# Decoder layer on one core: the self-attention values first, the weight splits moved, one output tile joined in halves, and six transpositions of the identity at the start

## The chip, the core and the metric

The kernel runs on one core of one Trainium2 chip. The metric is the time of one execution on the device in microseconds (us). The engines are TensorE (PE in the profile, its weight loads PEld), VectorE (DVE), ScalarE (ACT), GpSimd (POOL) and SyncE (SP), which only issues DMAs. Each runs its own instructions in the order in which they are written and meets the others through semaphores.

## What is computed

A post-norm decoder layer for x of 2 x 256 rows of 512 and a context of 2 x 512 rows of 512, in float32. Cut to its core:

```python
# self-attention: 32 heads of 16, causal, with ALiBi
qkv = x @ w_attn + b_attn; q, k, v = split(qkv)
scores = q k^T / 16 + slope * (key - query), masked; attn = softmax(scores)
x = layernorm(x + (attn @ v) @ w_proj + b_proj)
# cross-attention: 32 query heads of 128, 8 key/value heads, keys from [context, x]
q = rms_norm(x @ Wq); k = rms_norm(kv @ Wk); v = kv @ Wv
x = layernorm(x + (softmax(q k^T / sqrt(128)) @ v) @ Wo)
# feed-forward per head of 32, on permuted columns
x = layernorm(x + unpermute(gelu(permute(x) @ up) @ down))
```

## The kernel before

Precision is kept by splitting a float32 matrix into a rounded high half and the rest as low half; one product is then three matmuls (`three_passes`, L46): high by high, high by low, low by high. Here a **triple** is such a set of three matmuls of 128x128 by 128x512. Four triples give a 128x512 result in one of the eight PSUM banks. ScalarE writes high halves (`weights_hi`), VectorE or GpSimd low halves (`early_lo`, `late_lo`).

**Start** (`self_attention_and_keys`, L213). SyncE loads the four row tiles of x (L351), then weights in groups of four 256 KB pieces numbered p: w_attn's queries (p = 0), keys (1), values (2), Wk in two halves (3, 4), Wv in two (5, 6), w_proj (7), Wq (8, 9). There is one raw buffer of four pieces, so a piece of group p is issued when the low half of the same piece of p - 1 is made (L339 to L343). TensorE transposes all of x (L802, 16 transpositions), waits for the last low half of x (L804), then does queries and keys (2 x 16 triples, the loop at L805), then walks a list.

**The list** is made by `order_of_work` (L82) and walked by all engines. Its entries: S c, the scores of a quad of four heads (16 quads, L833); E (c, i), the shift on VectorE (L628) and the exponential on ScalarE (L485) of head i; R, the reciprocals of sums (L637) after which GpSimd normalises two heads (L421, L423) and makes the ALiBi bias of two heads of the next quad (L416); T, transposition of a head's probabilities (L854) and its copy by VectorE (L643); PV, the product with the values (L866); V j, the values of row tile j (four triples); CT and CX, transposition and split of a tile of context (L876, L621); "part" (n, r), an eighth of the cross-attention keys and values of row n: two triples; KG and KT, copying and transposing those keys; W p, the split of weight group p. S c + 1 may not start before the shifts of all four heads of quad c are done (s_out, L835). T and the context transpositions share two banks in turn, bank 4 and bank 7: a use waits until the one two uses back is drained.

In the list the four V entries stand between the exponentials of quad 0; the parts begin after S 1, five to each quad.

**Cross-attention** (L1071 on) does eight key/value heads in turns of four units. In a unit TensorE transposes probabilities (T a, L1580), multiplies by values (O a) and, between them, does "fillers", among them the output product W tt of row tile tt with four triples. T, W and others share a ring of banks 4 to 6 (`Turn`, L1003). In the last turn (`LAST_FILLERS`) W 1 stands at the end of the last unit, after O 5; then come W 2, the transposition of row tile 0 (L1553), half of W 3, that of row tile 1, the other half. VectorE adds each to x (L1433) and makes the layer norm (L1436 to L1444).

**Feed-forward** (L1620 on) begins on TensorE at L1902: it waits for the permutation matrix, for the ring, and for `xt_lo` 2 (the low halves of row tiles 0 and 1, L1450), transposes row tile 2 (L1837) and permutes the columns by matmuls (L1849, L1850).

## Time and profile before

| | |
|---|---|
| runs of the kernel | 844.33, 845.17, 846.02 us; median 845.17 |
| the profiled execution | 845.65 us, its span 843.8 us |
| PE busy | 826.2 us (98%) |
| DVE, ACT, POOL busy | 547.2, 474.9, 521.9 us |
| DMA | 56.22 MB, mean 67 GB/s |

The span is what the profile covers; 1.85 us of the execution lie outside it. The trace's times count from the span's start. A matmul's duration is modelled and overlaps the next one's start, so the distance between the starts of two is what one costs the engine.

### The profile page before, as it was taken

What the parts mean: (1) busy time and instruction counts of PE and PEld (TensorE: products, weight loads), DVE (VectorE), ACT (ScalarE), POOL (GpSimd) and SP (SyncE); (2) the same over time, 40 slices, a digit from 0 to 9 for tenths busy, and PEclk for the clock granted to TensorE, in tenths of its full rate; (3) what the DMA queues carried; (4) which work ended last, traced back from release to release, by engine and by line L of the source; (5) the groups of instructions that cost most, each with busy time, mean ns of one, the idle gap of its engine ahead of it and who ended that gap; (6) DMA issues with size and microseconds to landing.
All of it is one profiled execution on the core that took longest, in us unless ns stands there. A gap on an engine that the chain in (4) does not pass through costs nothing.

```text
span 843.8 us, 15130 instructions
## 1 busy us (share of the span) xinstructions
PE 826.2 (98%) x4851; PEld 694.6 (82%) x4851; DVE 547.2 (65%) x1507; ACT 474.9 (56%) x1006; POOL 521.9 (62%) x676
## 2 busy tenths in 40 slices
PE   7999999999999999999999999999999999999997
PEld 5777777777788888888888888888888888888874
DVE  4456566766355677667767676667666766677664
ACT  4666665566246656455555555556555555556554
POOL 3477876757336576766666756775676576636931
PEclk9999999999999999999999999999999999999999
DMA  6613223221141721112102112122121101100101
GB/s 202 197 51 113 80 72 114 63 72 56 50 138 51 243 80 46 51 60 67 50 19 87 27 61 68 37 68 68 37 68 68 37 2 24 58 0 1 26 1 50
DMA packets 48511, 56.22 MB, mean 67 GB/s; under 512 B 4671, under 2 KB 29773, under 8 KB 48461
## 3 DMA queue, kind: packets, MB, share of 16 engines
q1 hardware_dynamic: 48460, 55.59, 21.6%
q8 instruction: 27, 0.44, 0.2%
q14 instruction: 24, 0.19, 0.1%
HBM read 41.95 MB, written 13.63 MB: 66 GB/s over the span
## 4 chain that ended last, share of the span: by engine, by line
PE 61%; DVE 3%; ACT 2%; POOL 0%; issue 0%; POOLq 0%
PE bank L1534 15%; PE bank L48 11%; PE bank L50 11%; PE bank L49 11%; PE bank L1580 9%; PE bank L1524 1%; ACT prob L1349 1%; DVE x_mx L1420 1%; ACT prob L1724 1%; DVE pT_lo L1469 0%; PE bank L1849 0%; PE bank L1850 0%; PE bank L1881 0%; PE bank L1891 0%; PE bank L1890 0%
## 5 line engine op out<-in xcount | busy, mean ns | idle before, releaser
L1251 POOL TENSOR_SCALAR prob<-prob,x_rinv 128x768 f32<-128x768 f32 x124 | 112.5, 908 | 167.4 <-DVE x_rinv L1429 167.4
L1366 ACT ACTIVATE pT_hi<-bank 128x512 fp32r<-128x512 f32 x192 | 114.2, 597 | 90.3 <-PE bank L1580 89.9
L1349 ACT ACTIVATE prob<-bank,x_nm,q_rms 128x768 f32<-128x768 f32 x124 | 123.2, 994 | 47.1 <-DVE x_nm L1423 46.7
L1469 DVE TENSOR_TENSOR pT_lo<-bank,pT_hi 128x512 fp32r<-128x512 f32 x192 | 130.3, 679 | 5.1 <-ACT pT_hi L1366 3.7
L1420 DVE TENSOR_REDUCE x_mx<-bank 128x1 f32<-128x768 f32 x124 | 118.3, 954 | 22.0 <-PE bank L1534 21.7
L1580 PE MATMUL bank<-ident,prob 128*128 128x128 f32 x768 | 114.8, 272 | 2.1 <-POOL prob L1251 1.3
L1580 PEld LDWEIGHTS bank<-ident,prob 128*128 128x128 f32 x768 | 95.0, 140 | 14.1 <-POOL prob L1251 2.0
L48 PE MATMUL bank<-pT_hi,xv_hi 128*128 128x512 f32 x192 | 86.5, 450 | 1.2 <-DVE pT_lo L1469 0.9
L485 ACT ACTIVATE s_self<-s_self,nm_self 128x128 f32<-128x128 f32 (+1 forms) x128 | 57.1, 447 | 43.0 <-DVE nm_self L628 42.5
L50 PE MATMUL bank<-pT_hi,xv_lo 128*128 128x512 f32 x192 | 75.7, 394 | 0.0
L49 PE MATMUL bank<-pT_lo,xv_hi 128*128 128x512 f32 x192 | 75.4, 393 | 0.0
L1534 PE MATMUL bank<-xk_hi,qT_hi 128*128 128x384 f32 x244 | 65.6, 350 | 0.3 <-ACT prob L1349 0.2
L1534 PE MATMUL bank<-xk_lo,qT_hi 128*128 128x384 f32 x244 | 63.4, 341 | 0.0
L1534 PE MATMUL bank<-xk_hi,qT_lo 128*128 128x384 f32 x244 | 62.7, 337 | 0.0
L48 PE MATMUL bank<-wq_hi,x_hi 128*128 128x512 f32 x144 | 58.8, 408 | 0.0
L1375 ACT ACTIVATE oT_hi<-bank 128x512 fp32r<-128x512 f32 x32 | 19.1, 598 | 69.5 <-PE bank L50 69.4
L50 PE MATMUL bank<-wq_hi,x_lo 128*128 128x512 f32 x144 | 56.5, 393 | 0.0
L49 PE MATMUL bank<-wq_lo,x_hi 128*128 128x512 f32 x144 | 56.4, 392 | 0.0
L48 PE MATMUL bank<-w_hi,cT_hi 128*128 128x512 f32 x128 | 56.0, 438 | 0.0
L643 DVE COPY pT_self<-bank 128x384 f32<-128x384 f32 x64 | 35.4, 554 | 29.3 <-PE bank L854 29.0
L48 PE MATMUL bank<-wo_hi,oT_hi 128*128 128x512 f32 x128 | 52.3, 409 | 0.0
L1534 PEld LDWEIGHTS bank<-xk_hi,qT_hi 128*128 128x128 f32 x244 | 43.5, 189 | 9.4 <-ACT prob L1349 1.5
(233 smaller groups left out, 2047.8 us busy)
## 6 DMA issues: line engine op xcount, KB each, us to landing
wo_raw<-in_Wo SPq DMA_DIRECT2D x8, 1024.0 KB, 5.4
v_by_head<-v_st SPq DMA_DIRECT2D x12, 512.0 KB, 3.5
kT_by_head<-kT_st SPq DMA_DIRECT2D x12, 512.0 KB, 3.2
xk_raw<-kT_by_head SPq DMA_DIRECT2D x16, 384.0 KB, 3.2
xv_raw<-v_by_head SPq DMA_DIRECT2D x16, 384.0 KB, 3.2
wq_raw<-in_Wq SPq DMA_DIRECT2D x6, 1024.0 KB, 5.5
wq_raw<-in_w_attn SPq DMA_DIRECT2D x12, 256.0 KB, 4.3
xk_raw<-in_ctx SPq DMA_DIRECT2D x8, 256.0 KB, 2.6
```

What stands on the lines that cost most here:

```text
L48: nc.tensor.matmul(out, a_hi, b_hi, start=first, stop=False)
L49: nc.tensor.matmul(out, a_hi, b_lo, start=False, stop=False)
L50: return nc.tensor.matmul(out, a_lo, b_hi, start=False, stop=last)
L485: nc.scalar.activation(s_sb[:, c % 2, i, a:e], s_sb[:, c % 2, i, a:e], ACT.Exp, bias=nm[:, c % 2, i, qt:qt + 1], scale=-1.0, accum_out=rsu ...
L643: nc.vector.tensor_copy(pT[:, c % 2, i, :], bank[:, bank_of("T", (c, i)), 0:3 * P]).then_inc(pt_out, 1)
L1251: nc.gpsimd.tensor_scalar(prob[:, s, :], prob[:, s, :], rinv[:, s:s + 1], 1.0, ALU.mult, ALU.mult)\
L1349: nc.scalar.activation(prob[:, s, :].rearrange("p (a e) -> p a e", a=2), bank[:, at:at + 2, 0:HALF], ACT.Exp, bias=nm[:, s:s + 1], scale=q ...
L1366: nc.scalar.activation(pT_hi[:, a, :], bank[:, turn.bank[s, what, a], :], ACT.Copy)\
L1420: nc.vector.reduce_max(mx[:, s:s + 1], bank[:, at:at + 2, 0:HALF], AX.XY)\
L1469: nc.vector.tensor_tensor(pT_lo[:, a, :], bank[:, turn.bank[s, what, a], :], f32(pT_hi[:, a, :]), ALU.subtract).then_inc(ring_out, 1)
L1534: last = nc.tensor.matmul(bank[:, at + c, 0:HALF], a_hi[:, g, w], k_part[:, b, c * HALF:(c + 1) * HALF], start=start, stop=stop)
L1580: last = nc.tensor.transpose(bank[:, at, j * P:(j + 1) * P], prob[:, UT * (s % 2) + j, a * P:(a + 1) * P], ident[:])
```

## The change

It makes these edits. (1) SyncE issues x and the weights of the values in turn (x 0, piece 0, x 1, ...), and the value weights come first; the context tile 0 is loaded before the key weights. (2) On TensorE the values are computed first, piece by piece between the row transpositions, with waits for one tile and one piece each instead of for all; six transpositions of the identity into bank 7, read by nobody, stand between those of row tiles 0 and 1. Queries and keys follow. (3) ScalarE and VectorE split x and the first weight group in turn. Groups 3 and 5 move from GpSimd to VectorE. (4) The values leave the list; the first four parts take their place between the exponentials of quad 0. In exchange the odd quads among the first eight lose one part each. From the group of S 9 on the list is as it was. (5) In the last turn W 1 becomes two halves in bank 3, outside the ring: WA (two triples) after T 1 of the last unit, WB after O 5. (6) In the feed-forward the wait for `xt_lo` 2 stands behind the transposition of row tile 2.

```diff
-    order = [("S", 0), ("W", 5), ("V", 0), ("E", (0, 0)), ("V", 1), ("E", (0, 1)), ("V", 2), ("E", (0, 2)), ("CT", 0), ("CX", 0), ("V", 3),
-             ("E", (0, 3)), ("R", (0, 0)), ("W", 6), ("R", (0, 1))]
+    order = [("S", 0)]
...
+    for i in range(QUAD):
+        parts(1)
+        order.append(("E", (0, i)))
+        if i % 2:
+            order.append(("R", (0, i // 2)))
+    order.append(("W", 6))
...
-        if c < NQ - 1:
+        if c not in (1, 3, 5, 7, NQ - 1):
             parts(1)
...
-        ON_VECTOR, ON_POOL = (0, 1, 2, 4, 6, 8), (3, 5, 7)
+        ON_VECTOR, ON_POOL = (0, 1, 2, 3, 4, 5, 6, 8), (7,)
...
-                name, g = (("w_attn", 0), ("w_attn", 1), ("w_attn", 2), ("Wk", 0), ("Wk", 1), ("Wv", 0), ("Wv", 1),
+                name, g = (("w_attn", 2), ("w_attn", 0), ("w_attn", 1), ("Wk", 0), ("Wk", 1), ("Wv", 0), ("Wv", 1),
                            ("w_proj", 0), ("Wq", 0), ("Wq", 1))[p]
                 for i in range(KT):
-                    if p > 0 and p - 1 in ON_VECTOR:
+                    if p == 0:
+                        sp.dma_start(x[:, i, :], d["x"].rearrange("b s d -> (b s) d")[tokens(i), :]).then_inc(x_in[i], 16)
+                    elif p - 1 in ON_VECTOR:
                         sp.wait_ge(w_los, KT * ON_VECTOR.index(p - 1) + i + 1)
...
             for j in range(TT):
                 act.wait_ge(xt_ps, j + 1)
                 nc.scalar.activation(xT_hi[:, :, tokens(j)], bank[:, j, :].rearrange("p (k t) -> p k t", k=KT), ACT.Copy)\
                     .then_inc(xt_hi, 1)
-            for i in range(KT):
-                weights_hi(0, i)
...
+                weights_hi(0, j)
             for i in range(KT):
                 weights_hi(1, i)
+            act.wait_ge(zeros, 2)
+            for j in range(TT):
+                take_values_of(j)
...
+            def values(i, j):
+
+                pe.wait_ge(xt_lo, j + 1)
+                pe.wait_ge(w_los, i + 1)
+                last = three_passes(nc, bank[:, 4 + j, :], xT_hi[:, i, tokens(j)], xT_lo[:, i, tokens(j)],
+                                    w_hi[:, 0, i, :], w_lo[:, 0, i, :], i == 0, i == KT - 1)
...
+            row_transposes(0)
+            for _ in range(6):
+                nc.tensor.transpose(bank[:, 7, 0:P], ident[:], ident[:])
+            row_transposes(1)
+            values(0, 0)
+            row_transposes(2)
+            for i, j in ((0, 1), (1, 0), (1, 1)):
+                values(i, j)
+            row_transposes(3)
+            for i, j in ((0, 2), (1, 2), (2, 0), (2, 1), (2, 2), (0, 3), (1, 3), (2, 3)):
+                values(i, j)
+            for j in range(TT):
+                values(KT - 1, j)
...
 LAST_FILLERS = ((("W", 2), ("QT", 2), ("QT", 3), None),
                 (("W", 3), None, None, None),
                 (None, None, None, ("W", 0)),
-                (None, None, None, ("W", 1)))
+                (("WA", 1), None, None, ("WB", 1)))
...
+            def second_output(heads):
+                pe.wait_ge(o_out, UNITS * (KVH - 1) + 2)
...
             pe.wait_ge(k.matrix_made, KT)
             pe.wait_ge(k.ring_out, k.ring_drained)
-            pe.wait_ge(xt_lo, 2)
...
             transposes(2)
+            pe.wait_ge(xt_lo, 2)
             permute(free[0], 0)
```

**Where instructions move.** TensorE at the very start; `x_rows` is x, `x_hi` and `w_hi` are halves of x and of a weight group. Before:

```order
L802 MATMUL bank<-ident,x_rows 128x128 x16
L48 MATMUL bank<-x_hi,w_hi 128x512
L49 MATMUL bank<-x_lo,w_hi 128x512
L50 MATMUL bank<-x_hi,w_lo 128x512
L48 MATMUL bank<-x_hi,w_hi 128x512
```

Now:

```order
L846 MATMUL bank<-ident,x_rows 128x128 x4
L861 MATMUL bank<-ident 128x128 x6
L846 MATMUL bank<-ident,x_rows 128x128 x4
L48 MATMUL bank<-w_hi,x_hi 128x512
L49 MATMUL bank<-w_lo,x_hi 128x512
L50 MATMUL bank<-w_hi,x_lo 128x512
L846 MATMUL bank<-ident,x_rows 128x128 x4
L48 MATMUL bank<-w_hi,x_hi 128x512
L49 MATMUL bank<-w_lo,x_hi 128x512
```

The first product now stands behind two row tiles' transpositions and the six of the identity.

TensorE in the last unit of the cross-attention, from its first transpositions (`prob`) on. Before:

```order
L1580 MATMUL bank<-ident,prob 128x128 x12
L48 MATMUL bank<-pT_hi,xv_hi 128x512
L49 MATMUL bank<-pT_lo,xv_hi 128x512
L50 MATMUL bank<-pT_hi,xv_lo 128x512
L1580 MATMUL bank<-ident,prob 128x128 x4
```

Now:

```order
L1647 MATMUL bank<-ident,prob 128x128 x8
L48 MATMUL bank<-wo_hi,oT_hi 128x512
L49 MATMUL bank<-wo_lo,oT_hi 128x512
L50 MATMUL bank<-wo_hi,oT_lo 128x512
L48 MATMUL bank<-wo_hi,oT_hi 128x512
L49 MATMUL bank<-wo_lo,oT_hi 128x512
L50 MATMUL bank<-wo_hi,oT_lo 128x512
L1647 MATMUL bank<-ident,prob 128x128 x4
L48 MATMUL bank<-pT_hi,xv_hi 128x512
L49 MATMUL bank<-pT_lo,xv_hi 128x512
```

Two triples of the output product of row tile 1 now stand before O 0 (the product of `pT_hi` and `xv_hi`); its other two stay behind O 5.

## Rows read from the trace of the kernel before

**Rows 1.** The page, busy time, share of the span, instructions of TensorE and its loads.

```profile
PE 826.2 (98%) x4851; PEld 694.6 (82%) x4851; DVE 547.2 (65%) x1507; ACT 474.9 (56%) x1006; POOL 521.9 (62%) x676
PEclk9999999999999999999999999999999999999999
```

**Rows 2.** Waits of TensorE: line, who it waited for, us in total, times, longest.

```profile
PE bank L802 <- DMA x_rows<-in_x: 3.4, 1, 3.4
PE bank L48 <- DVE w_lo L617: 2.1, 1, 2.1
...
PE bank L48 <- DVE pT_lo L1469: 0.9, 2, 0.8
```

**Rows 3.** Timeline, TensorE, first 20 us: start, us, engine, line, tiles.

```profile
3.45 3.73 PE L802 MATMUL bank<-ident,x_rows 128*128 128x128 f32 x16 [3.45 <-DMA x_rows<-in_x]
9.28 0.77 PE L48 MATMUL bank<-x_hi,w_hi 128*128 128x512 f32 x1 [2.10 <-DVE w_lo L617]
9.84 0.63 PE L49 MATMUL bank<-x_lo,w_hi 128*128 128x512 f32 x1
10.27 0.63 PE L50 MATMUL bank<-x_hi,w_lo 128*128 128x512 f32 x1
...
15.47 0.40 PE L49 MATMUL bank<-x_lo,w_hi 128*128 128x512 f32 x1
15.72 0.40 PE L50 MATMUL bank<-x_hi,w_lo 128*128 128x512 f32 x1
...
17.12 0.40 PE L50 MATMUL bank<-x_hi,w_lo 128*128 128x512 f32 x1
```

**Rows 4.** Timeline, ScalarE, the first high halves.

```profile
4.57 0.60 ACT L524 ACTIVATE x_hi<-bank 128x512 fp32r<-128x512 f32 x1 [2.54 <-PE bank L802]
...
7.70 2.18 ACT L474 ACTIVATE w_hi<-wq_raw 128x512 fp32r<-128x512 f32 x4
```

**Rows 5.** Timeline, VectorE, the first low halves.

```profile
5.20 0.69 DVE L675 TENSOR_TENSOR x_lo<-bank,x_hi 128x512 fp32r<-128x512 f32 x1 [3.63 <-ACT x_hi L524]
...
8.45 2.49 DVE L617 TENSOR_TENSOR w_lo<-wq_raw,w_hi 128x512 fp32r<-128x512 f32 x4
```

**Rows 6.** Busy time of each engine, clock, DMA share and GB/s, 2 to 8 us.

```profile
2.00:8.00 6.00, 3.73 (x16) 3.11 (x16) 2.23 (x4) 2.61 (x6) 5.26 (x7) 1.00 0.99 343
```

**Rows 7.** Timeline, VectorE, quads 0 to 2: group 6's and a context tile's low halves, a last shift.

```profile
49.90 2.83 DVE L617 TENSOR_TENSOR w_lo<-wq_raw,w_hi 128x512 fp32r<-128x512 f32 x4 [1.94 <-ACT w_hi L474]
...
61.30 0.68 DVE L621 TENSOR_TENSOR cT_lo<-bank,cT_hi 128x512 fp32r<-128x512 f32 x1
...
65.94 0.42 DVE L628 CUSTOM_DVE_ANT_0 s_self<-bank,alibi 128x256 f32<-128x256 f32 x1
```

**Rows 8.** Timeline, TensorE, scores of quads 2 and 3, a transposition of quad 4.

```profile
58.16 0.94 PE L844 MATMUL bank<-kT_even,qT 32*128 32x128 f32 x16 [0.52 <-DVE nm_self L628]
...
68.32 0.94 PE L844 MATMUL bank<-kT_odd,qT 32*128 32x128 f32 x16
...
98.68 0.55 PE L854 MATMUL bank<-ident,s_self 128*128 128x128 f32 x3 [0.25 <-POOL s_self L423]
```

**Rows 9.** Timeline, GpSimd, w_proj's low halves ahead of quad 4's second normalisation.

```profile
92.79 5.02 POOL L408 TENSOR_TENSOR wq_lo<-wq_raw,wq_hi 128x512 fp32r<-128x512 f32 x4
```

**Rows 10.** Timeline, TensorE, end of the cross-attention and the feed-forward's first rows.

```profile
793.09 1.47 PE L1580 MATMUL bank<-ident,prob 128*128 128x128 f32 x12
795.35 0.47 PE L48 MATMUL bank<-pT_hi,xv_hi 128*128 128x512 f32 x1 [0.79 <-DVE pT_lo L1469]
...
811.12 0.63 PE L1837 MATMUL bank<-ident,x_rows 128*128 128x128 f32 x4 [0.62 <-DVE x_lo L1450]
811.50 0.36 PE L1849 MATMUL bank<-x_hi,wq_hi 128*128 128x256 f32 x1
```

**Rows 11.** Timeline, VectorE, output of row tile 2 added, last low half.

```profile
806.90 0.69 DVE L1433 TENSOR_TENSOR x_rows<-bank,x_rows 128x512 f32<-128x512 f32 x1 [0.57 <-PE bank L50]
...
810.17 0.68 DVE L1450 TENSOR_TENSOR x_lo<-bank,x_hi 128x512 fp32r<-128x512 f32 x1
```

More of the change, by code:

```diff
@@ L283, in self_attention_and_keys @@
         RING, GROUPS = (4, 7), (5, 6)
-        before = {4: ("V", 0), 7: ("V", 3), 5: ("V", 1), 6: ("V", 2)}
-        place, quad, rows_over = {}, 0, {}
+        before = {4: ("K", 0), 7: ("K", 3), 5: ("K", 1), 6: ("K", 2)}
+        place, quad, rows_over = {("CT", 0): (1, None)}, 0, {}
         ring_uses = 0
@@ L520, in copy_keys, with take_values_of @@
                 nc.scalar.activation(k_sq[:], k_rows[:, w, :], ACT.Square).then_inc(ksq_made, 1)
+            def take_values_of(j):
+                act.wait_ge(v_ps, j + 1)
+                for odds in range(2):
+                    lanes = slice(odds * SA_DIM, (odds + 1) * SA_DIM)
+                    nc.scalar.activation(padded[odds][:, j, :, lanes],
+                                         bank[:, 4 + j, :].rearrange("p (g e) -> p g e", e=2 * SA_DIM)[:, :, lanes],
+                                         ACT.Copy).then_inc(v_out, 1)
             for j in range(TT):
@@ L676, in _, with odd_keys @@
                                         f32(xT_hi[:, :, tokens(j)]), ALU.subtract).then_inc(xt_lo, 1)
-            for p in range(2):
-                for i in range(KT):
-                    early_lo(p, i)
+                early_lo(0, j)
+            for i in range(KT):
+                early_lo(1, i)
+            def odd_keys(m):
+                dve.wait_ge(qk_ps, KT + m + 1)
+                dve.wait_ge(k_out, m + 1)
+                nc.vector.tensor_scalar(kT_odd[:, m, :], bank[:, 4 + m, :], cols[:, KT + m:KT + m + 1],
+                                        odd[:], ALU.add, ALU.mult).then_inc(k_odd_out, 1)
+            for i in range(KT):
+                early_lo(2, i)
             dve.wait_ge(col_out, 1)
@@ L685, in _ @@
             for i in range(KT):
-                early_lo(2, i)
-            for m in range(KT):
-                dve.wait_ge(qk_ps, KT + m + 1)
-                dve.wait_ge(k_out, m + 1)
-                nc.vector.tensor_scalar(kT_odd[:, m, :], bank[:, 4 + m, :], cols[:, KT + m:KT + m + 1],
-                                        odd[:], ALU.add, ALU.mult).then_inc(k_odd_out, 1)
-                early_lo(4, m)
+                early_lo(3, i)
+            early_lo(4, 0)
+            context_lo(0)
+            for i in range(1, KT):
+                early_lo(4, i)
+            odd_keys(0)
+            early_lo(5, 0)
+            early_lo(5, 1)
+            odd_keys(1)
+            early_lo(5, 2)
+            early_lo(5, 3)
+            odd_keys(2)
+            odd_keys(3)
             for what, a in ORDER:
@@ L796, in drained, with context_transposes, row_transposes @@
                     pe.wait_ge(vg_late, i[0] + 1)
-            pe.wait_ge(const, 4)
-            for j in range(TT):
+            def context_transposes(n):
+                pe.wait_ge(c_in, 16 * (n + 1))
+                if n > 0:
+                    drained("CT", n)
+                for i in range(KT):
+                    last = nc.tensor.transpose(bank[:, bank_of("CT", n), tokens(i)], c_raw[:, tokens(i)], ident[:])
+                last.then_inc(ct_ps, 1)
+            def row_transposes(j):
                 pe.wait_ge(x_in[j], 16)
@@ L870, in weigh_values @@
                 last.then_inc(o_ps, 1)
-            def context_transposes(n):
-                pe.wait_ge(c_in, 16 * (n + 1))
-                drained("CT", n)
-                for i in range(KT):
-                    last = nc.tensor.transpose(bank[:, bank_of("CT", n), tokens(i)], c_raw[:, tokens(i)], ident[:])
-                last.then_inc(ct_ps, 1)
             def key_transposes(n, g):
@@ L912, in _ @@
             for what, a in ORDER:
-                if what == "V":
-                    values(a)
-                elif what == "S":
+                if what == "S":
                     scores(a)
```

123 lines of the change are left out of this document (70 added, 53 removed).

## The prediction

> **What bounds the kernel now.** The page comes first: TensorE is busy 826.2 of 843.8 us, no other engine over 65% [rows 1]. So time can only come from three places: TensorE's waits, matmuls run slower than they could be, and work removed. The change removes no work (and adds six transpositions), so I look for the other two. The list of TensorE's waits says where it stands still: 3.4 us for the first tile of x, 2.1 us for the first low half of a weight, 0.9 us in two waits for a low half of the probabilities [rows 2], and 0.6 us ahead of the feed-forward [rows 10].
>
> The timeline of the start shows the other loss. From 9.84 to 10.27 one matmul of 512 columns costs 0.43 us; from 15.72 to 17.12 six cost 1.40 us, 0.235 us each [rows 3]. These are the two levels of the clock: 512 columns take 0.427 us at 1.2 GHz and 0.213 us at 2.4 GHz. The granted clock of the stretch reads full [rows 1, 6], so it is the spacing that tells the level. TensorE works on transpositions from 3.45 to 7.18, stands until 9.28, then multiplies at the low level; the first matmul of 0.40 us starts at 15.47. I put the rise at 15.2, 5.9 us after work resumed. The stretch from 9.28 to the rise costs nearly twice its work.
>
> All times below are those of the one profiled execution: 845.65 us, with a span of 843.8. It is 0.48 us above the median of the three runs, 845.17, which themselves lie 1.7 us apart.
>
> **1. The start: -3.8 us.** The yardstick is when TensorE has 48 of the 144 projection matmuls behind it, all x transposed. Before: 12 ran at the low level, two more are issued by 15.72, and the other 34 at 0.235 are 8.0, so 23.7.
>
> Now, step by step. The first tile of x is there at 3.45 as before, since it is still issued first. From 2 to 8 us the DMAs move 343 GB/s [rows 6], 0.77 us for each 256 KB, so w 0 is due near 4.2, x 1 near 5.0, w 1 near 5.7, x 3 near 8.0, w 3 near 8.8. Sixteen transpositions took 3.73 us, 0.21 apiece beside a short gap [rows 3]: four for x 0 end at 4.3, the six of the identity at 5.6, x 1's at 6.45. Meanwhile ScalarE rounds x 0 at 4.57 (0.60 us) and w 0 (2.18 / 4 = 0.55 us) until 5.75 [rows 4], VectorE makes both low halves (0.69 and 2.49 / 4 = 0.62 us) until 6.5 [rows 5]. The first product starts at 6.6, not 9.28. x 1's low half follows near 8.1, w 1's near 8.7, and the rest of both keeps ahead of TensorE, which multiplies or transposes without a gap: one triple costs 1.28 us at the low level, 0.70 at the high one.
>
> The six transpositions cost nothing themselves: without them TensorE would wait from 5.2 to 6.6 for the same low half. What they may buy is the clock, and that is the choice of this term. If unbroken work of any kind counts, 5.9 us after 3.45 is 9.35: one triple ends at 7.9, x 2's transpositions at 8.7, 1.4 further matmuls at 9.35, and the other 43.6 x 0.235 plus 0.35 for x 3 end at 19.9: 23.7 - 19.9 = **3.8**. If only the products count, 5.9 us after 6.6 is 12.5: 11.8 matmuls are done, 36.2 x 0.235 + 0.35 end at 21.35: 2.35 us. If the count starts anew behind x 2's transpositions (8.7), 14.6 and 1.3 us. At best the rise comes near 7.2 and the products only wait for low halves: x 1's at 8.1, three triples until 10.2, x 3 and 36 matmuls until 19.0: 4.7 us. The trace has 3.7 us of transpositions at the low level without a rise, and then a stop; it does not decide. I take 3.8, because in the one rise that it shows, work had gone on for 5.9 us, and now work goes on from 3.45. Range 1.3 to 4.7.
>
> The Trainium skill (TensorE: Matmul & The Clock Gate, Part 4, PE-mode transpose) speaks against this: transposition does not count as busy for the clock. By it the six are worthless for the clock, the term is 2.35 us or less, and the sum below would be 843.35. No row here contradicts it: 3.7 us of transpositions did not raise the clock.
>
> The loads behind do not stop it: queries need group 1 split by 20 us, and its pieces can be issued from 6.5 us on, two microseconds sooner than before. The low halves of groups 3 and 5 add 8 x 0.69 = 5.5 us [rows 5] to VectorE while TensorE does 32 triples (22.6 us); nothing waits for them there, so they are at no price. If they had no cover, keys or parts would start late by as much.
>
> **2. The first eight quads: +1.2 us.** Their parts are only moved. What changes is how much work stands between a quad's scores and the next, and so what it covers.
> (a) Quad 0. Between S 0 and S 1 stood 16 triples, 11.3 us; now four parts, 5.6 us. Below them run the last odd keys, four shifts, exponentials, and now a key copy, its square and its sum ahead of the last shift: by my count the last shift ends 6.9 us after S 0 begins, TensorE is there at 6.5: 0.4 us. Then VectorE makes group 6's low halves (2.83 us [rows 7]) between quad 0's last shift and the first copy of its transposed probabilities. T (0,1) shares bank 4 with T (0,0), since CT 1 took bank 7 between: it waits some 0.8 us for that copy. Before, this stretch lost about as much less 0.4, among it 0.52 us at S 2 [rows 8]. Net +0.4.
> (b) The odd quads lose a part, 6 x 0.235 = 1.41 us, between the last T and the next S. In quad 2 the last shift ended at 66.36 and S 3 began at 68.32, 1.96 us later [rows 7, 8]: 0.55 are left. Ahead of S 5 VectorE has in addition a key sum and a low half of context (0.68 us [rows 7]) before its last shift. I take 0.6 us there and 0.2 at S 7 or S 9.
> (c) w_proj's low halves hold GpSimd 5.02 us [rows 9] ahead of the second normalisation of quad 4; T (4,2) waited 0.25 us for it [rows 8]. The first normalisation now starts a key transposition and a part later against S 5; I take a stall of 0.5 more. Part of it falls into S 5's own wait, so (b) and (c) give +0.8 together.
> Lower bound of the term: 0, if the slack suffices. Upper bound: 2.6 (0.8 + 0.6 + 0.2 + 1.0).
>
> **3. The end: -1.15 us.** Twelve transpositions from 793.09 take 12 x 0.09, until 794.2; O 0 starts at 795.35 [rows 10]. 1.15 us are idle, of which the row shows 0.79 as a wait. WA, 6 x 0.235 = 1.41 us, fills that and pushes O 0 to 795.55. Its inputs are long there: it reads units 0 and 1, and the exponentials that read bank 3 belong to the unit before. Behind O 5 only 1.41 us of W 1 are left instead of 2.8, so W 2 would start 1.2 us earlier; but it needs the low half of unit 3's output, made near 802.9. It starts at 803.0 and ends at 805.75. VectorE adds it at 806.1 instead of 806.90 [rows 11], and 0.8 us goes down the chain of normalisation and low halves. On TensorE the transposition of tile 2 then no longer waits for x_lo of tile 1 (810.17 + 0.68 [rows 11]): it starts near 809.7 instead of 811.12, and the permutation, which still needs that low half, near 810.35 instead of 811.50 [rows 10]: **1.15**. From there on the tail is the same work. Lower end 0.8 (the wait for the low half is what counts), upper end 1.4 (the whole filler).
>
> **Sum:** 845.65 - 3.8 + 1.2 - 1.15 = **841.9 us**, 3.3 below the median.
>
> **Rivals.**
> (A) Transpositions do not count for the clock. For: the 3.7 us without a rise. Against: that stretch ended in a stop, so it proves little. Time 845.65 - 2.35 + 1.2 - 1.15 = 843.35.
> (B) The moved parts cost nothing: the quads' slack holds and the clock rises earlier. For: the list of TensorE's waits puts hardly anything down to the quads [rows 2], and S 3 had 1.96 us to spare. 845.65 - 4.4 + 0 - 1.25 = 840.0.
> (C) Slower than before: the parts taken from the odd quads were the cover of the shift chain. GpSimd's normalisation, bias, then VectorE's shift decide when S may start; if they, not TensorE, set the pace in quads 1 to 8, each of the four missing parts turns into a wait: 4 x 1.41 = 5.6 us in place of (b). It decides once the last shift ends less than 1.41 us before S. With (a) and (c) at their upper ends: 845.65 - 2.35 + 5.6 + 1.8 - 0.8 = 849.9; at the sizes of the forecast 845.65 - 3.8 + 5.6 + 0.9 - 1.15 = 847.2. Against it: 1.96 us of slack at S 3, of which 0.55 are left. Chance 5%.
> (D) The change does not do what it says at the end: W 2's wait for unit 3's output gives all of it back. Then 1.15 shrinks to 0.5, and the time is 842.6, inside the range.
>
> **How the numbers follow.** Forecast (with D) 55%, A 25%, B 15%, C 5%. 841.9 is the forecast's. The range leaves out C and the edges: from B's 839.8 to A with the upper bounds of part 2 and 0.8 at the end, which is 844.6. A measurement of this kernel can tell 0.2%, 1.7 us. Faster means below 843.48: nearly all of the forecast (53%) and B (15%), and over half of A (14%), 0.82. Slower than 846.86 is C, 0.04. The rest is 0.14.
>
> **What would show it.** In the timeline of the start: first product near 6.6 us, no wait for `w_lo`, the first 0.235 us spacing near 9.4 (forecast) or 12.5 (A), the values done near 20. In the quads: waits of TensorE's scores for `nm_self` at S 1 and S 5, of T (0,1) for a copy, under 2.5 us together up to 130 us; C would show 1 us or more at each of S 3, S 5, S 7 and S 9. At the end: no wait for `pT_lo` ahead of O 0, and 0.3 us or so between the transposition of tile 2 and the permutation. The prediction is wrong if the products wait for splits between 7 and 20 us, or if the queries wait for group 1.

## The result, and the profile after

The change makes the kernel **slower**: 849.52 us, the median of 8 runs (847.8 to 850.76), against 845.4 (843.11 to 846.43) for the kernel before in 8 runs on the same chip. The ratio is 1.0047, with a 95% interval of 1.0037 to 1.0057. The profiled execution took 850.76 us, the longest of the eight; its span is 849.0. It lies 5.1 us above the profiled execution of before, while the medians are 4.1 apart, and the sums below are those of the profiled executions. One execution of an experiment, the profiled one of e5, took 1465.05 us at a granted clock of 0.718, and nothing is read from it.

The page of the changed kernel, busy time, beside [rows 1]:

```profile
PE 827.1 (97%) x4857; PEld 695.6 (82%) x4857; DVE 554.7 (65%) x1515; ACT 475.7 (56%) x1006; POOL 513.9 (61%) x668
```

Its busy time is 0.9 us up, the span 5.2: TensorE stands still more. (A time in which it does nothing is called a stand here.) Its waits by line, beside [rows 2]:

```profile
PE bank L846 <- DMA x_rows<-in_x: 3.9, 2, 3.6
PE bank L916 <- POOL s_self L429: 2.9, 2, 1.7
PE bank L916 <- DVE x_lo L671: 2.6, 1, 2.6
PE bank L906 <- DVE nm_self L650: 1.8, 3, 0.9
...
PE bank L938 <- DVE x_lo L671: 0.7, 1, 0.7
```

The waits for `w_lo` (2.1) and `pT_lo` (0.9) are gone. Three lines that the list of before did not lead with have come: L916 is the transposition T of a tile of a quad's probabilities, L906 the scores S, L938 the key transposition KT. They add 8.0 us.

**The start.** TensorE's timeline, beside [rows 3]:

```profile
3.58 1.09 PE L846 MATMUL bank<-ident,x_rows 128*128 128x128 f32 x4 [3.58 <-DMA x_rows<-in_x]
4.46 1.49 PE L861 MATMUL bank<-ident 128*128 128x128 f32 x6
6.30 1.12 PE L846 MATMUL bank<-ident,x_rows 128*128 128x128 f32 x4 [0.35 <-DMA x_rows<-in_x]
7.07 0.78 PE L48 MATMUL bank<-w_hi,x_hi 128*128 128x512 f32 x1
...
9.20 0.72 PE L48 MATMUL bank<-w_hi,x_hi 128*128 128x512 f32 x1
9.76 0.40 PE L49 MATMUL bank<-w_lo,x_hi 128*128 128x512 f32 x1
...
20.22 0.40 PE L50 MATMUL bank<-w_hi,x_lo 128*128 128x512 f32 x1
```

The products begin at 7.07 and not at 9.28, the product at 9.20 is the last of 0.56 us spacing; from 9.76 on they take 0.40 and not from 15.47, and the last product of the values starts at 20.22 and is paid at 20.45: 3.25 us ahead of the 23.7 of the kernel before.

**The quads.** The loss lies between S 1 and S 9. TensorE's timeline, its stands from 40 to 150 us but for one of 0.26 at T (4,3), 108.43:

```profile
50.84 0.94 PE L906 MATMUL bank<-kT_odd,qT 32*128 32x128 f32 x16 [0.43 <-DVE nm_self L650]
...
56.78 0.52 PE L916 MATMUL bank<-ident,s_self 128*128 128x128 f32 x3 [1.27 <-POOL s_self L429]
...
77.89 0.80 PE L916 MATMUL bank<-ident,s_self 128*128 128x128 f32 x3 [2.62 <-DVE x_lo L671]
...
96.66 0.94 PE L906 MATMUL bank<-kT_odd,qT 32*128 32x128 f32 x16 [0.87 <-DVE nm_self L650]
...
105.79 0.55 PE L916 MATMUL bank<-ident,s_self 128*128 128x128 f32 x3 [1.66 <-POOL s_self L429]
...
119.65 0.94 PE L906 MATMUL bank<-kT_odd,qT 32*128 32x128 f32 x16 [0.53 <-DVE nm_self L650]
...
144.70 0.63 PE L938 MATMUL bank<-ident,k_rows 128*128 128x128 f32 x4 [0.73 <-DVE x_lo L671]
```

In the order of the program: S 1, T (0,1), T (2,0), S 5, T (4,2), S 7, and a KT in quad 9. The distances between the starts of scores put prices on them, here in us, with those of two experiments beside them:

| | before | after | e10 | e8 |
|---|---|---|---|---|
| S 1 to S 2 | 10.23 | 11.32 | 11.32 | 9.77 |
| S 2 to S 3 | 10.16 | 8.76 | 8.76 | 8.75 |
| S 3 to S 4 | 11.63 | **15.96** | 11.59 | 11.60 |
| S 4 to S 5 | 10.21 | 9.78 | 9.79 | 9.78 |
| S 5 to S 6 | 12.11 | **13.61** | 13.63 | 11.20 |
| S 6 to S 7 | 10.59 | 9.38 | 9.41 | 9.17 |
| S 7 to S 9 | 21.35 | 20.03 | 20.06 | 20.03 |
| S 1 to S 9 | 86.28 | 88.84 | 84.56 | 80.30 |

The kernel before does four parts more in this stretch, 4 x 1.41 = 5.64 us; everything else in it is the same in number. Its 86.28 are thus 80.64 of the same work, and the change loses 88.84 - 80.64 = **8.2 us** here. S 1's own wait, 0.43, lies ahead of its start and comes on top. S 9 to S 15 costs 0.68 more (the KT), the start gives 3.25 back and the end 0.95. Together that is +5.1, the distance of the two profiled executions (850.76 and 845.65). Of the 8.2, T (2,0) has 4.37. The other stands of the stretch add up to 4.59 (1.27, 0.87, 1.66, 0.26, 0.53), where the kernel before stood 1.0 (0.52, 0.23 and 0.25), and 0.2 is in no wait.

**T (2,0)** is the largest. The three timelines around it; TensorE, up to it and behind it:

```profile
74.88 0.40 PE L50 MATMUL bank<-w_hi,cT_lo 128*128 128x512 f32 x1
...
78.34 0.78 PE L48 MATMUL bank<-w_hi,cT_hi 128*128 128x512 f32 x1
...
80.62 0.63 PE L50 MATMUL bank<-w_hi,cT_lo 128*128 128x512 f32 x1
81.05 0.67 PE L916 MATMUL bank<-ident,s_self 128*128 128x128 f32 x3
```

ScalarE and VectorE:

```profile
75.88 0.40 ACT L489 ACTIVATE s_self<-s_self,nm_self 128x128 f32<-128x128 f32 x1 [1.37 <-DVE nm_self L650]
...
76.77 0.45 ACT L496 ACTIVATE x_hi<-bank,cols 128x256 fp32r<-128x256 f32 x1
```

```profile
74.55 0.69 DVE L643 TENSOR_TENSOR cT_lo<-bank,cT_hi 128x512 fp32r<-128x512 f32 x1 [1.21 <-ACT cT_hi L482]
...
77.26 0.48 DVE L671 SCALAR_TENSOR_TENSOR x_lo<-bank,cols,x_hi 128x256 fp32r<-128x256 f32 x1 [1.47 <-ACT x_hi L496]
```

T, PV, CT and KT take banks 4 and 7 in turn. In the list of before, PV 0 and T (2,0) were neighbours among these four and so on different banks; T (2,0) took the one of KT (0,0), and did not wait. The moved parts bring CT 2 between them. So T (2,0) takes the bank of PV 0, and that is emptied by AH 0 on ScalarE (76.77) and A 0 on VectorE (77.26), which stand in the list behind CX 2 and E (3,0): behind a context tile's halves, a shift and an exponential. TensorE reaches T (2,0) at 75.28 and starts at 77.89. Six products behind it cost 81.05 - 78.34 = 2.71 us; at 0.235 each they would cost 1.4. That is the clock at its lower level: products at 0.43 us, 1.2 GHz, after a stand of 2.6 us. The granted clock confirms it: 0.50 from 79.0 to 80.5 and 1.00 from 81.4 to 86.0, which makes 0.89 (the third figure from the end) from S 3 to S 4:

```profile
70.92:86.88 15.96, 13.35 (x100) 10.08 (x99) 8.04 (x29) 7.33 (x25) 8.74 (x19) 0.89 0.37 114
```

**KT (4,0), in quad 9,** waits for a copy of the same kind, that of PV 3's output, but no change of banks brought this. Both lists read PV 3, T (8,0), KT (4,0), so it takes the bank of PV 3 in both. What is late is the chain ahead of the copy. The first shift of E (9,0) on VectorE, before and now:

```profile
135.61 0.29 DVE L628 CUSTOM_DVE_ANT_0 s_self<-bank,alibi 128x128 f32<-128x128 f32 x1 [1.16 <-POOL alibi L416]
```

```profile
141.95 0.29 DVE L650 CUSTOM_DVE_ANT_0 s_self<-bank,alibi 128x128 f32<-128x128 f32 x1 [1.16 <-POOL alibi L422]
```

Both wait for the bias that GpSimd makes. The shift starts 1.40 us behind S 9 (134.21) before and 2.27 us behind S 9 (139.68) now, when no part stands between the last T of quad 7 and S 9. The copy of PV 3's output, which the list has behind E (9,0), ends 4.00 us behind S 9 before and 4.87 now. KT started right behind that end before; now it stands 0.73 us. That the missing part is the reason is read from the two timelines, and no run tries it by itself.

**T (0,1)** is named as waiting for GpSimd. It waits for two things that end together, one of them VectorE's. Beside [rows 7], group 6's low halves, then a shift, then the copy that empties the bank:

```profile
52.42 3.19 DVE L639 TENSOR_TENSOR w_lo<-wq_raw,w_hi 128x512 fp32r<-128x512 f32 x4 [0.34 <-ACT w_hi L478]
...
56.09 0.54 DVE L665 COPY pT_self<-bank 128x384 f32<-128x384 f32 x1
```

The copy ends at 56.63, GpSimd's normalisation for T (0,1) at 56.67, and T (0,1) starts at 56.78: either alone would have held it about as long. The normalisation is late because the two before it had taken 1.32 and 1.42 us beside that row of low halves, where others take 0.37 and 0.48:

```profile
53.15 1.32 POOL L427 TENSOR_SCALAR s_self<-s_self,rinv_self 128x128 f32<-128x128 f32 x1
54.46 1.42 POOL L429 TENSOR_SCALAR s_self<-s_self,rinv_self 128x256 f32<-128x256 f32 x1
55.86 0.36 POOL L427 TENSOR_SCALAR s_self<-s_self,rinv_self 128x128 f32<-128x128 f32 x1
56.20 0.47 POOL L429 TENSOR_SCALAR s_self<-s_self,rinv_self 128x256 f32<-128x256 f32 x1
...
99.90 5.03 POOL L414 TENSOR_TENSOR wq_lo<-wq_raw,wq_hi 128x512 fp32r<-128x512 f32 x4
```

The last row is **T (4,2)**: w_proj's low halves, beside [rows 9], end at 104.93, and T (4,2) starts at 105.79, when the first normalisation behind them is done.

**The end.** T 0 of the last unit starts at 799.24, beside the 793.09 of [rows 10], and tile 2's transposition follows 16.83 us later, where it took 18.03:

```profile
799.24 1.04 PE L1647 MATMUL bank<-ident,prob 128*128 128x128 f32 x8
...
816.07 0.63 PE L1908 MATMUL bank<-ident,x_rows 128*128 128x128 f32 x4
```

From T 0 to the end of the span it is 49.76 us, before 50.71: 0.95 less.

### The profile page after: what moved, and what is told of

The parts are those of the page before. It is cut to its first block, busy times and chain, and to the rows that moved or that the text cites. A ratio compares the mean times of both kernels' runs of the same rounds, so it can differ in the third digit from the quotient of the medians.

```text
span 849.0 us, 15156 instructions
## 1 busy us (share of the span) xinstructions
PE 827.1 (97%) x4857; PEld 695.6 (82%) x4857; DVE 554.7 (65%) x1515; ACT 475.7 (56%) x1006; POOL 513.9 (61%) x668
## 3 DMA queue, kind: packets, MB, share of 16 engines
HBM read 41.95 MB, written 13.63 MB: 65 GB/s over the span
## 4 chain that ended last, share of the span: by engine, by line
PE 61%; DVE 2%; ACT 2%; issue 0%; POOL 0%; POOLq 0%
PE bank L1590 15%; PE bank L48 11%; PE bank L50 11%; PE bank L49 11%; PE bank L1647 9%; PE bank L1580 1%; ACT prob L1404 1%; DVE x_mx L1475 1%; ACT prob L1795 1%; PE bank L1920 0%; PE bank L1921 0%; DVE pT_lo L1524 0%; PE bank L1952 0%; PE bank L1962 0%; PE bank L1961 0%
## 5 line engine op out<-in xcount | busy, mean ns | idle before, releaser
L427 POOL TENSOR_SCALAR s_self<-s_self,rinv_self 128x128 f32<-128x128 f32 x64 | 24.8, 387 | 49.5 <-DVE rinv_self L659 49.0
```

## The experiments

All times are medians, each beside the kernel before on the same chip; an interval of the ratio is some 0.1% to either side, 0.8 us, so a difference between two kernels is taken from their ratios or medians and from their profiles together.

**e1: the output of a pair copied at once** (the changed kernel, and AH and A right behind PV; a second way to the same bank order is e10).

```diff
-            order.append(("PV", c // 2 - 1))
+            order += [("PV", c // 2 - 1), ("AH", c // 2 - 1), ("A", c // 2 - 1)]
...
-            if late:
-                order.append(("AH", c // 2 - 1))
...
-            if pair and i == 0:
-                if not late:
-                    order.append(("AH", c // 2 - 1))
-                order.append(("A", c // 2 - 1))
```

> The changed kernel, with the eviction of the attention output (AH on ScalarE, A on VectorE) put right behind PV in the list instead of behind a part and the next quad's first exponential. Theory 'bank': TensorE's wait of 2.6 us at T(2,0) is for the bank that PV 0 holds, because CT 2 now stands between PV 0 and T(2,0) and takes the other bank; it is released only after that eviction, and the stand brings the clock down (another 1.4 us). Then T(2,0) waits no longer, the matmuls behind it stay at 0.235 us, the wait of 0.7 us at the key transposition of quad 9 shrinks too, and the time falls by 3.5 to 4.7 us to about 845.3. Theory 'cover' (the odd quads lack a part that hid the softmax chain): the wait only moves to the next scores, and the time stays within 1 us of 849.5.

Measured: 844.84 us, ratio 1.0002 (0.9993 to 1.0012), span 843.8. The stands of T (2,0) and of KT are gone and so is the low clock; the others stay (S 1 0.43, T (0,1) 1.28, S 5 0.87, T (4,2) 1.74, T (4,3) 0.26, S 7 0.54). S 0 to S 15 costs 156.54 us in place of 161.85. With two entries of the list moved, the change costs nothing against before.

**e10: the same for the first pair alone.**

```diff
             order.append(("PV", c // 2 - 1))
+            if c == 2:
+                order += [("AH", 0), ("A", 0)]
```

> The changed kernel with a single entry moved: the copies of the first pair's output (AH 0 on ScalarE, A 0 on VectorE) stand right behind PV 0, as in e1; those of the other pairs stay where the change has them. Theory 'the bank of PV 0 behind CT 2 is the main loss': T(2,0)'s 2.6 us and the low clock behind it (1.4) go with this entry alone, 849.52 - 4.0 = 845.5, and KT's wait of 0.73 us near 144 stays, which e1 also took away. Rival 'early copies help all pairs alike, a little each': e1's 4.7 us are spread over seven pairs and this kernel gains 0.7 us or less, 848.8.

Measured: 846.08 us, ratio 1.0008 (0.9999 to 1.0017), 3.4 us below the changed kernel's median. TensorE's timeline at T (2,0):

```profile
75.79 0.49 PE L918 MATMUL bank<-ident,s_self 128*128 128x128 f32 x3
76.03 0.48 PE L48 MATMUL bank<-w_hi,cT_hi 128*128 128x512 f32 x1
...
77.51 0.49 PE L918 MATMUL bank<-ident,s_self 128*128 128x128 f32 x3
...
141.13 0.63 PE L940 MATMUL bank<-ident,k_rows 128*128 128x128 f32 x4 [0.77 <-DVE x_lo L673]
```

No stand, the six products between at 0.25 us (1.48 in all), and KT's wait as it was, 0.77 us. S 3 to S 4 falls from 15.96 to 11.59: **4.4 us hang on one bank**, 2.62 as the stand and 1.75 as what TensorE does at the low clock behind it. The two profiled executions are only 3.5 us apart, because this one reached S 0 at 44.48 and not at 43.81: x 1 came 0.24 us later, and the clock rose at 10.8, not 9.7. The medians are 3.4 apart; the runs of either kernel scatter by 2 us and more, so they cannot check the 4.4 more closely.

**e11: the early copies in the kernel before** (e1's edit, made to the kernel before).

> The kernel before the change, with AH and A of every pair right behind their PV, as in e1. In it T(2,0) has no wait, since CT 2 does not stand between PV 0 and T(2,0). Theory 'the early copies only cure what the change broke': no difference, ratio 0.999 to 1.001. Rival 'they are worth something by themselves', so that e1's gain is no evidence for the bank: 2 us or more faster, 843 or less.

Measured: 845.02 us, ratio 0.9999 (0.999 to 1.0008). The early copies are worth nothing by themselves. They cure what the change brought in.

**e2: without the six transpositions of the identity.**

```diff
-            for _ in range(6):
-                nc.tensor.transpose(bank[:, 7, 0:P], ident[:], ident[:])
```

> The changed kernel without the six transpositions of the identity. Theory 'any work counts': TensorE stands still from 4.5 to 6.3 us, the clock rises one to three us later than 9.6 us, and the time is 1 to 2 us longer than the changed kernel's. Theory 'transpositions do not count': the rise stays where it was, give or take its scatter, and the time is within 0.5 us of 849.5.

Measured: 850.95 us, ratio 1.0077 (1.0061 to 1.0094): 1.4 us by the medians above the changed kernel. By the ratios it is 2.5 us, with some 1.6 to either side. The first product starts at 6.82 behind a wait of 0.59 us for `w_lo`, and the high level comes near 10.1, not 9.7. T (2,0) stands 2.63 us here too. The runs have the six worth something, but the two profiles do not show it: S 0 is at 43.88 here and at 43.81 with the six, and both spans are 849.0 us. The rise did not come one to three us later, as the first theory had it.

**e4: the six transpositions in the kernel before**, behind those of the rows, where TensorE stood 2.1 us for `w_lo`.

```diff
                 last.then_inc(xt_ps, 1)
+            for _ in range(6):
+                nc.tensor.transpose(bank[:, 7, 0:P], ident[:], ident[:])
```

> The kernel before with six transpositions of the identity into bank 7 behind the row transpositions, in the stand of 2.1 us ahead of the first product. Theory 'any work counts': TensorE stands only 0.8 us, the clock rises at about 9.5 to 12.5 us instead of 15.2, and 1.3 to 2.8 us are gained. Theory 'transpositions do not count': no change beyond 0.3 us.

Measured: 843.2 us, ratio 0.9984 (0.9974 to 0.9994), span 841.8. TensorE's timeline has nothing but transpositions ahead of the first product, and that product already has the short spacing:

```profile
7.69 1.49 PE L805 MATMUL bank<-ident 128*128 128x128 f32 x6
10.00 0.47 PE L48 MATMUL bank<-x_hi,w_hi 128*128 128x512 f32 x1 [0.82 <-DVE w_lo L617]
10.31 0.39 PE L49 MATMUL bank<-x_lo,w_hi 128*128 128x512 f32 x1
```

Transpositions count for the clock; e3, next, shows it without the six. The Trainium skill (TensorE: Matmul & The Clock Gate, Part 4, PE-mode transpose) says that they do not; this trace contradicts it, and rival A falls with it. The gain, 1.4 us by the ratio, is clear of noise. It is not shown to come from an earlier rise, for e3 has the high level at its first product too.

**e3: the edits of the end alone, in the kernel before.**

> The kernel before with the edits of the end alone (WA and WB in bank 3, the wait for xt_lo behind the transposition of row tile 2). Theory 'the end gains by itself': 1.15 us by the prediction, 0.95 us by the two traces: 844.4 against 845.4. Rival 'the end's gain hangs on the rest': no difference.

Measured: 843.77 us, ratio 0.9992 (0.9982 to 1.0002), 0.7 us less with 0.8 to either side: a gain of the size that the traces show (0.95), but by itself not told apart from none. In its profile, T 0 of the last unit to the end of the span takes 49.69 us, 1.0 less than before.

The same profile bears on the clock. The start of this kernel is that of the kernel before, without the six transpositions of the identity:

```profile
9.30 0.47 PE L48 MATMUL bank<-x_hi,w_hi 128*128 128x512 f32 x1 [2.10 <-DVE w_lo L617]
9.61 0.40 PE L49 MATMUL bank<-x_lo,w_hi 128*128 128x512 f32 x1
...
10.80 0.63 PE L48 MATMUL bank<-x_hi,w_hi 128*128 128x512 f32 x1
```

Its first product, behind 16 transpositions and the stand of 2.10 us, already has the short spacing, where the kernel before had the long one in its profile [rows 3]. Six products later the level falls; the granted clock is 0.51 from 10.70 to 14.10 us and then 0.99. So one and the same start runs at either level at its first product, and a stand of 2.10 us was followed by the low level, 1.4 us after its end.

**e5: w_proj's low halves one at a time** (e1, and one piece behind the second normalisation of each of quads 3 to 6).

```diff
         if more:
             order.append(("R", (c + 1, 1)))
+        if 3 <= c < 7:
+            order.append(("WP", c - 3))
...
-                if what == "W" and a == 7:
-                    late_lo(a)
+                if what == "WP":
+                    pool.wait_ge(w_his, KT * 7 + a + 1)
+                    hi, lo = split_of(7, a)
+                    nc.gpsimd.tensor_tensor(lo, w_raw[:, a, :], f32(hi), ALU.subtract).then_inc(late_los, 1)
```

> The kernel of e1_out_early, with w_proj's four low halves on GpSimd one at a time behind the second normalisation of quads 3 to 6, in place of all four in a row (5.03 us) ahead of the second normalisation of quad 4. Theory 'GpSimd's row of four blocks the path': the waits of T(4,2), 1.74 us in e1, and of T(4,3), 0.26 us, go, and S5's own wait stays at 0.87 since it stands ahead; the spread pieces (1.25 us each) lie behind a normalisation and cost nothing. S 15 starts 1.5 to 2.0 us earlier than in e1 (200.5 to 198.5-199.0), time 843.0 to 843.4 against e1's 844.84. Rival 'the alibi's shift on VectorE would have come late anyway': T(4,2) still waits over 1 us, now for VectorE, and the time is 844.5 or more.

Measured: 842.11 us (842.02 without the execution of 1465.05), ratio 0.9968 (0.9955 to 0.998), 2.9 us below e1 by the ratios where 1.5 to 2.0 were expected. There is no profile to read; e8 shows the place instead.

**e6: group 6 split among quad 0's exponentials** (e1, and this).

```diff
+    order += [("H6", 0), ("H6", 1), ("H6", 2)]
     for i in range(QUAD):
         parts(1)
         order.append(("E", (0, i)))
+        if i == 1:
+            order += [("L6", 0), ("L6", 1)]
+        if i == 2:
+            order += [("H6", 3), ("L6", 2)]
+        if i == 3:
+            order.append(("L6", 3))
...
-    order.append(("W", 6))
```

> The kernel of e1_out_early, with group 6's splits moved out of the gap between quad 0's last shift and the copy of its transposed probabilities: three high and then its low halves one by one between the exponentials and shifts of quad 0, ahead of its first part. Theory 'VectorE's row of four low halves is what T(0,1) waits for, and it slows GpSimd's normalisations': the wait of T(0,1), 1.28 us in e1, falls below 0.3; GpSimd's two normalisations beside the row (1.32 and 1.42 us each) come back towards 0.4 to 0.5 where no low half runs beside them, but S 1's wait for the last shift (0.43 us) grows to up to 1.0 because some low halves now stand ahead of shifts. Net 0.7 to 1.2 us, time 843.6 to 844.1 against e1's 844.84. Rival 'the normalisation itself, slow or not, is what T(0,1) waits for': T(0,1) still waits 0.8 us or more and the time is that of e1.

Measured: 843.74 us, ratio 0.9985 (0.9975 to 0.9994), 1.1 us below e1 by the medians. T (0,1) does not wait, S 1 waits 0.89 us. GpSimd, ahead of T (0,1), has its usual durations back:

```profile
53.13 0.38 POOL L427 TENSOR_SCALAR s_self<-s_self,rinv_self 128x128 f32<-128x128 f32 x1
```

The normalisation at 48.31, beside the low half that VectorE makes at 48.23, took 0.85 us: the slowness follows the low halves. Which of the two late things alone would have held T (0,1), the copy or the normalisation, this edit does not separate, for it moves both.

**e7: the parts left out later** (e1, parts left out behind quads 11 to 14).

```diff
-        if c not in (1, 3, 5, 7, NQ - 1):
+        if c not in (11, 12, 13, 14, NQ - 1):
```

> The kernel of e1_out_early, with the parts left out behind quads 11 to 14 instead of behind 1, 3, 5 and 7; the number of parts is the same. Theory of small prices (my parts b): the missing part before S5 and S7 costs 0.87 and 0.54 us; both waits go with the part back, T(4,2)'s 1.74 us shrinks too since the first normalisation of quad 4 then has 1.41 us more, and late quads, whose S wait for nothing in e1, keep 0.2 to 0.5 us of new waits each. Time 0.5 to 2.0 us below e1's 844.84, that is 842.8 to 844.3. Rival C, 'every missing part is a wait of 1.4 us': 4 x 1.4 go at the front and 4 x 1.4 come behind, with S 9 5 us earlier than in e1 and S 15's end no earlier; the time is e1's.

Measured: 848.64 us, ratio 1.0044 (1.0029 to 1.006): 3.8 us **slower** than e1 by the medians (3.5 by the ratios), outside both expectations. Its timeline has lost the stands of S 5, S 7 and T (4,2), 3.15 us, as the theory of small prices had it, and has new ones:

```profile
149.09 0.50 PE L48 MATMUL bank<-w_hi,cT_hi 128*128 128x512 f32 x1 [1.25 <-DVE v_st L673]
...
158.01 0.50 PE L48 MATMUL bank<-w_hi,cT_hi 128*128 128x512 f32 x1 [1.05 <-ACT v_st L505]
...
175.11 0.94 PE L900 MATMUL bank<-kT_even,qT 32*128 32x128 f32 x16 [1.22 <-DVE x_lo L751]
...
185.34 0.94 PE L900 MATMUL bank<-kT_odd,qT 32*128 32x128 f32 x16 [1.34 <-DVE x_lo L751]
```

With three more of 0.56, 0.23 and 0.54 that is 6.2 us. Parts ahead of their place meet work that has not moved with them: a part waits for a copy of values, a score for a low half of a row tile, a transposition for a copy of keys. By their releasers these are waits for a bank that is copied out late. Whether a new order of the banks brought them, as at T (2,0), or work that stayed behind, was not followed.

**e9: e5, e6 and e7 together.**

> The edits of e5, e6 and e7 together on the kernel of e1_out_early. If the three waits are separate places, the gains add up: 1.7 + 1.0 + about 1.0, less what T(4,2)'s wait has in both e5 and e7 (0.5), so 3.2 us below e1: 841.6, range 840.8 to 842.8, which is faster than the kernel before the change. If TensorE's stands only move from one place to the next, it stays at 843.5 or above.

Measured: 847.06 us, ratio 1.0024 (1.0015 to 1.0034), 1.6 us below e7 and far above the 840.8 to 842.8 that were expected. The first quads are clean but for S 1's 0.90 us, and the late stands are those of e7 (1.25, 1.05, 1.23, 1.34 among them).

**e8: e5 and e6 on e1.**

> e1_out_early with the edits of e5 (w_proj's low halves one by one behind quads 3 to 6) and of e6 (group 6's splits between the exponentials of quad 0), parts left out behind 1, 3, 5, 7 as in the change. e5 gave 2.7 us and e6 1.1 us against e1. If the two stands are separate places the sum is 844.84 - 2.7 - 1.1 = 841.0, range 840.4 to 841.8, and of the waits up to 130 us S 1's (0.9), S 5's (0.9) and S 7's (0.5) are left. If e5's gain beyond the 2.0 us of its two waits was something else, for instance an earlier normalisation for S 5, S 5's wait is smaller here than in e1. Should it come out at 842 or above, one of the two only moved the stand of the other.

Measured: **840.62 us**, 6 runs from 840.41 to 842.21, ratio 0.9953 (0.9941 to 0.9965), span 838.6. It is the fastest kernel of the study, 4.0 us below the kernel before by the ratio. All stands up to 200 us behind the start:

```profile
49.96 0.94 PE L914 MATMUL bank<-kT_odd,qT 32*128 32x128 f32 x16 [0.90 <-DVE nm_self L656]
...
89.86 0.94 PE L914 MATMUL bank<-kT_odd,qT 32*128 32x128 f32 x16 [0.88 <-DVE nm_self L656]
...
110.23 0.94 PE L914 MATMUL bank<-kT_odd,qT 32*128 32x128 f32 x16 [0.33 <-DVE nm_self L656]
```

GpSimd's timeline in quad 4, one piece, behind the last normalisation (102.44):

```profile
103.97 1.30 POOL L444 TENSOR_TENSOR wq_lo<-wq_raw,wq_hi 128x512 fp32r<-128x512 f32 x1
```

T (4,2) and T (4,3) wait no more; S 5 to S 6 falls from 13.61 to 11.20. The wait of S 7 shrinks from 0.53 to 0.33. S 1 to S 9 costs 80.30 us, 0.3 less than the kernel before without its four parts (80.64). S 0 to S 15 costs 152.90 us, 8.95 less than in the changed kernel, and the medians are 8.9 apart.

**e12: e8 with the parts left out behind 1, 7, 9 and 11.**

```diff
-        if c not in (1, 3, 5, 7, NQ - 1):
+        if c not in (1, 7, 9, 11, NQ - 1):
```

> The kernel of e8_spread_w6, with the parts left out behind quads 1, 7, 9 and 11 instead of 1, 3, 5 and 7. From e7: with the parts back behind 3 and 5 the waits of S 5 (0.87) and S 7 (0.54) go, but with the feed-forward's units four parts ahead of their place e7 had new stands of 6.2 us from 149 us on. Here they are two parts ahead at most between quads 3 and 9. If the new stands of e7 come from being three or four ahead, this gives e8's time less 1.4: 839.6, range 839.2 to 840.8. If any part moved ahead brings a stand behind it (the same bank or context copy comes late), it is e8's time or up to 2 us more.

Measured: 842.83 us, ratio 0.9977 (0.9967 to 0.9986), 2.2 us slower than e8. The waits of S 5 and S 7 go (1.2 us), and new ones come, a part at 151.32 for `v_st` (1.25), S 11 (0.36) and S 13 (1.34). Already two parts ahead are too many here; the second expectation holds.

## Why the prediction was wrong

The forecast was 841.9 with a range to 844.6; measured are 849.52, and 850.76 in the profiled execution, by which the sum was made.

The two ends of the range do not follow from its own terms. A with the upper bound of part 2 and 0.8 at the end is 845.65 - 2.35 + 2.6 - 0.8 = 845.1, not 844.6, and B's own sum is 840.0, not 839.8. The measured time is outside either way.

**Part 1, the start: the size is right, in part by luck.** -3.8 was predicted, -3.25 measured. The first product came at 7.07 for 6.6, above all since TensorE waited 0.35 us for x 1; no product waited for `w_lo`; the rise came at 9.7 for 9.35; the values were done at 20.45 for 19.9. Of the two theories of the clock, the right one was taken: work that is all transpositions does count (e4, e3). But the 5.9 us of unbroken work by which the rise was placed are no fixed time. In kernels with this very start the high level was there between 6.6 us or before and 10.8 us, 3.2 to 7.3 us after the first transposition. That 9.7 is near 9.35 is luck within that scatter. The sentence that the six "cost nothing themselves" agrees with e2, which is not faster without them.

**Part 3, the end: right.** -1.15 predicted, -0.95 measured; both waits went, for `pT_lo` and for `x_lo`, by the mechanism that was told.

**Part 2, the first eight quads: here it failed.** "+1.2 us" with an "upper bound 2.6"; measured 0.43 at S 1, +8.2 between S 1 and S 9, and +0.68 behind, 9.3 us in all. The step that failed is that every wait but the named ones was put at nothing: the banks given out in turn were followed at one place only, and T (2,0), which is 4.4 us (15.96 less 11.59 in e10), was not on the list. By its steps:
- (a) S 1 was given 0.4 and has 0.43. T (0,1) was given 0.8 and has 1.27. The place is as told. Of the cause one half was told, the copy behind the low halves; the slowed normalisation, which ends with it, was not. The four low halves took 3.19 us and not the 2.83 of [rows 7], and they began later than I had counted.
- (b) S 5 was given 0.6 and has 0.87; S 7 has 0.53, S 9 none, for 0.2 at one of them; the lateness at S 9 comes out at KT, with 0.73.
- (c) T (4,2) was given 0.5 more than its 0.25. It has 1.66, and 0.26 at T (4,3). Counted from S 5, the row on GpSimd ends 8.3 us later where it ended 7.7 (97.81 [rows 9] less S 5 at 90.16), and TensorE without the wait would be there after 7.5 and not after 8.3: 0.6 and 0.8 make the 1.4 us more. I had taken the first alone.
- Together the stands that were named come to 5.0 us, about twice what they were priced at, and a credit of 0.8 was taken for stands of before that the new ones were to replace.
- **What was not named at all is 4.4 us at T (2,0) and 0.7 at KT.** The prediction did look at the ring of two banks, at one place ("T (0,1) shares bank 4 with T (0,0), since CT 1 took bank 7 between"), and not at the others. Moving four parts moves CT and KT with them, and each one between two holders swaps the banks of all that follow. T (2,0) met a holder that is emptied late. (KT (4,0) is another matter: its bank has the same holder as before, which is emptied later.) And the stand costs more than its length, because the clock falls behind it: 1.75 us on top of 2.62. Part 1 had priced the clock's two levels with care for the start, and part 2 let no stand cost more than itself.
- The bound of 2.6 was a sum of the known stands at their upper ends. It was no bound on the stretch. [Rows 2] showed that the quads of before hardly waited, which I took for slack; it was an order in which everything fitted.

**The rivals.** A is refuted by e4 and e3. B had the slack hold; it did not. C comes nearest in time, 849.9 at its upper ends, and is wrong in mechanism: it wanted a wait of 1.4 us at each of S 3, S 5, S 7 and S 9, and they are 0, 0.87, 0.53 and 0. With KT's 0.73 behind S 9, what the missing parts laid bare is 2.1 us of the 5.6 that C wanted; that its time is within 0.4 us of the measured one is luck. D did not happen.

What stays open: 0.2 us between S 1 and S 9 that no wait carries, what the six transpositions are worth and by what, and which of the two late things at T (0,1) would have held it longer.

The places add up. From the changed kernel to e1 it is 4.7 us of median (T (2,0), its clock, KT), from there to e8 another 4.2 (T (4,2), T (0,1)), 8.9 in all, against the 8.9 of S 1 to S 15 that the change had lost. With them out of the way the time is 840.62, ratio 0.9953, where the forecast was 841.9. This does not confirm the forecast, which counted 1.2 us of loss in the quads. Nor are the 4.0 us below the kernel before shown to be all the change's: the edits of e5 and e6 were not tried on the kernel before, whose own stands in this stretch are 1.0 us.

## What to carry to other kernels

When work is moved in a list from which buffers are given out in turn, write down the holder of each buffer before and after, all the way to where the two lists agree again: one entry more or less between two users swaps everybody's predecessor. Price a stand of TensorE as long as those seen here (2.62 us, and 2.10 in e3) with the slower matmuls behind it. When a part is taken away, follow the chain past the next scores: at S 9 nothing waited, and the transposition behind it did. And empty a shared bank as the next thing after it is filled: in this kernel that costs nothing (e11), and it took away the stands of T (2,0) and KT (e1).

## What the runs showed of the hardware

- **Transpositions raise the clock.** In e4 and e3 only transpositions precede the first product (22 and 16), and it runs at the high level, 0.235 us per 512 columns.
- **The moment of the rise differs between profiles of kernels with the same work ahead of S 0**: 6.6 us or before (e12), 6.8 or before (e9), 7.2 (e8), 7.7 (e6), 9.3 (e7), 9.7 (after), 10.1 (e1), 10.8 (e10). The first and the last are 2 us of S 0 apart (42.49 and 44.48). The four early ones have e6's edit and the four late ones do not, but that edit touches nothing ahead of 20 us. The start of the kernel before, without it, varies as much: the low level up to 15 us or so in two profiles (before, e11), the high one from the first product in the third (e3). So I take it for chance. It was not tried.
- **A stand of 2.62 us brought the low level, those of 1.66 and 1.27 did not**: behind T (4,2) products go on at 0.23 us, from 106.85 to 107.08 and 107.32. One of 2.10 us, in e3, was followed by six fast products and then by 3.4 us at a granted clock of 0.51.
- **Ahead of the first rise the granted clock reads 1.00 though the level is low.** It does so from 12.00 to 15.20 in the kernel before, where the products are 0.43 us apart; the spacing tells the level there. Later falls show in it (0.51 in e3, 0.50 behind T (2,0)).
- **Beside VectorE's weight low halves GpSimd takes three times as long.** A normalisation of 0.37 us takes 1.32, one of 0.48 takes 1.42, while VectorE subtracts in 32-bit floats from one SBUF tile to another; the longest of VectorE's four low halves takes 1.29 us then, the shortest 0.68. The Trainium skill (GPSIMD Engine Reference, Specifications) says that the two share their SBUF interfaces, and contend where VectorE's instruction has two SBUF inputs; these low halves, w_raw less w_hi, have two, and the trace agrees, with 1.32 us for 0.37.
